# The deformable convolution of an eight-stage image network: a tap's spread products in row groups, and a new order of the stage

## The chip, the cores and the metric

The kernel runs on 1 core of one Trainium2 chip. The metric is the device time of one execution in microseconds. Before the change it is 1125.55 us, the median of 3 runs (1121.36 to 1129.44). Engines are named as the profile names them: PE is TensorE, DVE VectorE, ACT ScalarE, POOL GpSimd, SP SyncE.

## What is computed

Sixteen images of 16 x 16 pixels with 64 channels go through eight stages, each a residual on a normalized input. The change is in the third, a deformable 3 x 3 convolution. Its core in the reference:

```
om = lax.conv_general_dilated(x, om_kernel, (SH, SW), 'SAME', ...) + om_bias
off = om[..., :2 * DG * K].reshape(Bx, Ho, Wo, DG, K, 2)
mask = jax.nn.sigmoid(om[..., 2 * DG * K:]).reshape(Bx, Ho, Wo, DG, K) * 2.0
...
for yi, wy in ((y0, 1.0 - fy), (y0 + 1.0, fy)):
    for xi, wx in ((x0, 1.0 - fx), (x0 + 1.0, fx)):
        ...
        g = jnp.take_along_axis(xf, lin[..., None], axis=1)
        val = val + g * (wy * wx * valid.astype(x.dtype))[..., None]
cols = (val * mask_t[..., None]).reshape(Bx, Ho * Wo, K * Cx)
out = jnp.matmul(cols, kernel).reshape(Bx, Ho, Wo, -1) + bias
```

Each output pixel reads the image at nine shifted places (taps), each between four pixels. The other stages are a gate, a top-k feed-forward, three mixtures of experts, an attention and a plain 3 x 3 convolution whose kernel is divided by its spectral norm. That norm comes from 20 steps of a power iteration, of which each block of the third stage carries one.

## The kernel before

The images are worked in eight blocks of two images (512 pixels), in every stage. The code issues to each engine by hand, in the order in which it stands, and the engines meet at semaphores. `trips` runs a stage's body as a loop of three rounds of two blocks (u = 0 and 1) and a last round apart (wrap). While block b is worked, block b + 1 is prepared and the normalization of block b + 2 is begun.

The third stage gathers without addresses. For a tap, a pixel's weight on source pixel (y, x) is a product of two hats, max(0, 1 - |distance|) in y and in x. `hats_distances` (DVE) forms the distances for 16 rows and 16 columns, `hats_form` (ACT, L869 and L871) takes absolute value and hat, `hats_masked` multiplies the mask in. `hats_part` (ACT, L876), `hats_rest` and `hats_last` split the result into three bf16 parts in HB. `turn` (PE, L1265) turns two taps of HB, pixels to the free side, into bank 7; `ht_out` (ACT, L887) copies them to HT: 96 rows, three parts of 16 for y and three of 16 for x.

Then three products per tap spread a tap's 16 values to 256 source pixels: `spread_y` (L1273) makes two of 128 x 512 in a pair of banks, `spread_x` (L1269) one in bank 0. All three contract the same 96 rows against a 0/1 matrix `spread`. `xr_out` (ACT, L893) copies bank 0 to XR, `products` (DVE, L1902) multiplies the pair by XR into S. `gather` (PE, L1281) contracts S over the source pixels with Z, the image already multiplied by the tap's kernel (`z_tile`, L1257, copied by `z_out`, L881), and sums nine taps in bank 1. At a block's end the offsets of block b + 2 are made (`offsets`, L1236), copied (`offsets_out`) and turned (`turn_offsets`, L1242); the output is biased (L1948), turned back (`turn_output`, L1249) and added to X (L1950), which is block_done.

Two pairs of banks (2 and 3, 4 and 5) serve the y products, the z tiles and the offsets. Which pair a tap takes is a table:

```
TAP_PAIR = (1, 1, 0, 0, 1, 1, 0, 0, 1)
Z_PAIR = (1, 0, 1, 0)
```

PE spreads a tap in two steps, `tap(k)` for the y products and `x_of(k + 1)` for the next x product, with gathers, turns and z tiles between them, and the border of a block spreads tap 0 and the x part of tap 1 ahead. Between them stand `slot1`, `slot2` and `slot3` (L1096 to L1121), the small products of the power iteration, whose rest runs on POOL: `seg1`, `seg2`, `seg3`, `front` and, in even blocks, `split_later`, which splits weights for later stages.

## Time and profile before

| | us |
|---|---|
| median of 3 runs (lowest, highest) | 1125.55 (1121.36, 1129.44) |
| the profiled execution | 1133.36 |
| its span, first to last instruction | 1131.6 |
| PE busy | 933.4 (82%) |
| DVE busy | 695.3 (61%) |
| ACT busy | 492.1 (43%) |
| POOL busy | 444.7 (39%) |
| mean granted clock | 0.862 |

The profile is one execution. Times in its rows are microseconds from the span's start, where not marked ns. A share of busy time averages over eight stages with different limits. The third stage lies at about 230 to 530 us. Matmuls are pipelined: a record's duration contains the way through the array, so the starts of neighbours tell how long one held the engine. PEclk is the granted clock of TensorE as a share of its full speed. An f32 product appears as two records.

### The profile page before, as it was taken

What the parts mean: (1) busy time and instruction counts of PE and PEld (TensorE: products, weight loads), DVE (VectorE), ACT (ScalarE), POOL (GpSimd) and SP (SyncE); (2) the same over time, 40 slices, a digit from 0 to 9 for tenths busy, and PEclk for the clock granted to TensorE, in tenths of its full rate; (3) what the DMA queues carried; (4) which work ended last, traced back from release to release, by engine and by line L of the source; (5) the groups of instructions that cost most, each with busy time, mean ns of one, the idle gap of its engine ahead of it and who ended that gap; (6) DMA issues with size and microseconds to landing.
All of it is one profiled execution on the core that took longest, in us unless ns stands there. A gap on an engine that the chain in (4) does not pass through costs nothing.

```text
span 1131.6 us, 16666 instructions
## 1 busy us (share of the span) xinstructions
PE 933.4 (82%) x4266; PEld 558.4 (49%) x4266; DVE 695.3 (61%) x2439; ACT 492.1 (43%) x966; POOL 444.7 (39%) x1234
## 2 busy tenths in 40 slices
PE   2766486758999889889999976899897768999998
PEld 2655354545554545455444444556554544445443
DVE  2887677736455654564388857665875555656642
ACT  1324122246445653563266644343441013666664
POOL 4666566621542546336444401243555221111100
PEclk9999996559888988999799988776977666999999
DMA  4500000000000000000000000000000000000000
GB/s 74 91 1 1 1 1 0 0 1 1 1 1 0 0 0 0 0 1 1 1 1 1 0 1 0 1 1 0 0 1 1 0 0 1 6 5 9 5 6 9
DMA packets 26352, 6.21 MB, mean 5 GB/s; under 512 B 24068, under 2 KB 26244, under 8 KB 26308
## 3 DMA queue, kind: packets, MB, share of 16 engines
q1 hardware_dynamic: 26308, 5.70, 2.9%
q8 instruction: 18, 0.29, 0.1%
q14 instruction: 26, 0.21, 0.1%
HBM read 4.65 MB, written 1.05 MB: 5 GB/s over the span
## 4 chain that ended last, share of the span: by engine, by line
PE 51%; DVE 12%; issue 7%; ACT 3%; POOL 3%; DVEq 0%; POOLq 0%; ACTq 0%; another core or an unknown queue 0%
PE banks L1455 10%; PE banks L1281 6%; PE banks L1165 6%; PE banks L1166 4%; PE banks L1472 3%; PE banks L1096 3%; PE banks L1479 3%; PE banks L1423 2%; PE banks L1273 2%; DVE weighted L2007 2%; DVE V L1730 2%; DVE summed L2011 2%; PE banks L1429 1%; PE banks L1236 1%; PE banks L1269 1%
## 5 line engine op out<-in xcount | busy, mean ns | idle before, releaser
L646 POOL TENSOR_TENSOR rstd<-vareps,neghalf 128x4 f32<-128x4 f32 x64 | 66.8, 1044 | 274.4 <-DVE vareps L1714 269.5
L969 ACT ACTIVATE scratch<-banks,b 128x512 f32<-128x512 f32 x224 | 143.3, 682 | 52.5 <-PE banks L1166 39.9
L1455 PE MATMUL banks<-scratch,W 128*64 128x512 f32 (+1 forms) x448 | 149.3, 649 | 2.3 <-DVE weighted L2007 2.0
L1902 DVE TENSOR_TENSOR scratch<-banks,XR 128x1024 f32<-128x1024 f32 x72 | 87.5, 1224 | 87.4 <-PE banks L1273 61.1
L1165 PE MATMUL banks<-VS,W_hi 128*128 128x512 f32 x240 | 116.3, 485 | 2.1 <-DVE X L2083 1.0
L1166 PE MATMUL banks<-VS,W_lo 128*128 128x512 f32 x240 | 102.6, 427 | 0.0
L2007 DVE SCALAR_TENSOR_TENSOR weighted<-banks,b,cwide 128x512 f32<-128x512 f32 x72 | 54.0, 750 | 75.6 <-PE banks L1455 74.0
L1281 PE MATMUL banks<-scratch,region 128*64 128x256 f32 x576 | 87.4, 429 | 3.0 <-DVE scratch L1902 3.0
L980 ACT ACTIVATE cwide<-banks 128x512 f32<-128x512 f32 x96 | 57.5, 599 | 66.7 <-PE banks L1472 66.3
L1730 DVE TENSOR_SCALAR V<-X,moments,rstd 128x64 f32 (+1 forms) x256 | 67.7, 328 | 24.7 <-POOL rstd L646 22.0
L1165 PEld LDWEIGHTS banks<-VS,W_hi 128*128 128x128 f32 x240 | 49.1, 205 | 50.7 <-issue 26.1
L1139 PE MATMUL banks<-ident,V 128*128 128x128 f32 x128 | 34.3, 359 | 46.5 <-DVE V L1730 46.3
L742 ACT ACTIVATE VS<-banks 64x256 fp32r<-64x256 f32 x96 | 36.4, 379 | 77.5 <-PE banks L1139 61.2
L574 POOL TENSOR_TENSOR cp<-U,qv 64x18 f32<-64x18 f32 x40 | 8.1, 221 | 142.7 <-ACT U L800 142.7
L1281 PEld LDWEIGHTS banks<-scratch,region 128*64 128x64 f32 x576 | 38.0, 148 | 37.5 <-issue 22.3
L1757 DVE TENSOR_TENSOR VS<-banks,VS 64x256 fp32r<-64x256 f32 x96 | 40.5, 422 | 21.4 <-ACT VS L742 19.5
L1139 PEld LDWEIGHTS banks<-ident,V 128*128 128x128 f32 x128 | 16.4, 170 | 75.3 <-issue 42.1
L1455 PEld LDWEIGHTS banks<-scratch,W 128*64 128x64 f32 (+1 forms) x448 | 32.9, 150 | 40.7 <-issue 27.8
L1166 PEld LDWEIGHTS banks<-VS,W_lo 128*128 128x128 f32 x240 | 49.9, 208 | 6.1
L1472 PE MATMUL banks<-cwT,select 16*128 16x512 f32 x96 | 50.8, 529 | 0.8 <-ACT cwT L974 0.8
L2011 DVE TENSOR_TENSOR summed<-summed,weighted 128x512 f32<-128x512 f32 x72 | 49.9, 693 | 2.5
L887 ACT ACTIVATE HT<-banks 96x1024 bf16<-96x1024 bf16 (+1 forms) x40 | 37.2, 931 | 29.0 <-PE banks L1265 29.0
(289 smaller groups left out, 2008.3 us busy)
## 6 DMA issues: line engine op xcount, KB each, us to landing
W<-in_L_ffn_W SPq DMA_DIRECT2D x3, 512.0 KB
X<-in_x SPq DMA_DIRECT2D x8, 128.0 KB, 2.6
out<-X SPq DMA_DIRECT2D x8, 128.0 KB, 2.0
cwide<-in_L_ffn_W SPq DMA_DIRECT2D x2, 256.0 KB
KC<-in_L_conv_kernel SPq DMA_DIRECT2D x2, 144.0 KB
W<-in_L_ffn_W SPq DMA_DIRECT2D x1, 256.0 KB
cwide<-in_L_ffn_w SPq DMA_DIRECT2D x2, 128.0 KB
Ko<-in_L_conv_w SPq DMA_DIRECT2D x1, 144.0 KB, 3.7
```

The costliest lines, as they stand in the source:

```text
L646: pool.tensor_tensor(rstd[:], vareps[:], neghalf[:], ALU.pow).then_inc(rstd_ready, 1)
L969: act.activation(hid[:, c % 4, :], bank[c % 2][:, :], ACT.Gelu, bias=b1[s][:, w:w + 1]).then_inc(h_ready, 1)
L980: act.activation(cwide[:, j, :], bank[4][:, :], ACT.Copy).then_inc(wide_copied, 1)
L1165: pe.matmul(out, hi, VS[u][:], start=True, stop=False)
L1166: return pe.matmul(out, lo, VS[u][:], start=False, stop=True)
L1281: ins = pe.matmul(bank[1][m * C:(m + 1) * C, 0:PIX], Z[v][:, 2 * m + h, k * C:(k + 1) * C], S[:, k % 3, h, m * PIX:(m + 1) * PIX], start=( ...
L1455: ins = pe.matmul(y, W2[s][:, w, :], hid[:, c % 4, :], start=opens, stop=closes, skip_group_check=True)
L1472: pe.matmul(bank[4][:, :], select[:, j, :], cwT[:], start=True, stop=True).then_inc(wide_psum, 1)
L1730: ins = vec.tensor_scalar(V[u][:, place, :], X[:, bass.ds(b * NT + t, 1), :].rearrange("p o c -> p (o c)"), moments[:, t, 0:1], rstd[:, t: ...
L1902: vec.tensor_tensor(S[:, k % 3], pair(p), xr, ALU.mult).then_inc(s_ready, 1)
L2007: vec.scalar_tensor_tensor(weighted[:] if j else summed[u][:], bank[2 + j % 2][:, :], b2[s][:, j:j + 1], cwide[:, j, :], ALU.add, ALU.mult ...
L2011: add = vec.tensor_tensor(summed[u][:], summed[u][:], weighted[:], ALU.add)
```

## The change

The hats lie in four groups instead of two: y rows 0 to 7, y rows 8 to 15, x 0 to 7, x 8 to 15, each with three parts of 8 and a gap of 8 to make 32. HB and HT so have 128 rows, of which the gaps are filled with zeros once, on ACT. `spread` is one matrix of 128 x 128. A tap's three products now contract different rows: y's first half rows 0 to 31, the second 32 to 63, x rows 64 to 127. They are issued together (`spread_tap`), two taps ahead of the gather, and tap k takes the pair (u + k) % 2, as does the z tile that follows it. The offsets and the turned offsets go to bank 7. At the program's start POOL makes the grids with eight iotas of eight columns where there were four of sixteen, and `spread` with twelve selects where there were nine. `slot1` and `slot2` are cut in two parts with a gather between them. The orders of PE, ACT, DVE and POOL are rewritten; the border spreads taps 0, 1 and 2 of the next block (9, 10 and 11 in the code). The buffers `rest`, `weighted` and `summed` share one piece of memory.

The diff, cut, with eight spaces of the code's indent taken out:

```
-spread = sb("spread", [HAT, 3, P], BF16)
+spread = sb("spread", [P, P], BF16)
...
-hats = sb("hats", [P, 2, NT * TAPS, IMG])
-rest = sb("rest", [P, 2, NT * TAPS, IMG])
+hats = sb("hats", [P, 4, NT * TAPS, HALF])
+sums = sb("sums", [P, 3 * BLK])
+rest = view(sums, 0, (4, NT * TAPS, HALF))
 offs = sb("offs", [P, NT, 2 * TAPS])
-HB = [sb(f"HB{u}", [P, NT * TAPS, HAT], BF16) for u in range(2)]
-HT = sb("HT", [HAT, 2, 2, BLK], BF16)
+HB = [sb(f"HB{u}", [P, NT * TAPS, P], BF16) for u in range(2)]
+HT = sb("HT", [P, 2, 2, BLK], BF16)
...
-weighted = sb("weighted", [P, BLK])
-summed = [sb(f"summed{u}", [P, BLK]) for u in range(2)]
+weighted = sums[:, 0:BLK]
+summed = [sums[:, (u + 1) * BLK:(u + 2) * BLK] for u in range(2)]
...
-TAP_PAIR = (1, 1, 0, 0, 1, 1, 0, 0, 1)
...
+    by_pixel = spread[:].rearrange("r (y x) -> r y x", x=IMG)
     for q in range(PARTS):
-        for half_y in range(2):
-            v = spread[:, half_y, :].rearrange("r (y x) -> r y x", x=IMG)
+        for h in range(2):
+            link(pool.affine_select(out=by_pixel, in_=by_pixel, compare_op=ALU.not_equal, fill=1.0,
+                                    base=-(QUAD * h + HALF * q), pattern=[[-1, HALF], [0, IMG]],
+                                    channel_multiplier=1))
+            v = by_pixel[:, :, HALF * h:HALF * (h + 1)]
             link(pool.affine_select(out=v, in_=v, compare_op=ALU.not_equal, fill=1.0,
-                                    base=-IMG * q - 8 * half_y, pattern=[[-1, 8], [0, IMG]],
+                                    base=-(QUAD * (2 + h) + HALF * q), pattern=[[0, HALF], [-1, HALF]],
                                     channel_multiplier=1))
-        v = spread[:, 2, :].rearrange("r (y x) -> r y x", x=IMG)
-        link(pool.affine_select(out=v, in_=v, compare_op=ALU.not_equal, fill=1.0,
-                                base=-IMG * (PARTS + q), pattern=[[0, 8], [-1, IMG]],
-                                channel_multiplier=1))
...
-            if s != 2 and first_half:
+            if s == 2:
+                front()
+            if first_half:
                 seg1(step)
+            if u == 0 and s == 2:
+                rewind()
+                split_later(i, s, wrap)
             if first_half:
                 seg2(step)
             if second_half:
                 seg3(step)
             if second_half:
-                if not (s == 5 and wrap):
+                if s == 0 or s == 2 and wrap and u == 1 or s in (1, 5) and not wrap:
                     front()
                 rewind()
-            if u == 0 and s in (2, 6):
+            if u == 0 and s == 6:
...
+        for u in range(2):
+            gaps = HB[u][:].rearrange("p n (a r) -> p (n a) r", a=4)[:, :, PARTS * HALF:]
+            act.activation(gaps, ones[:, 0:1].rearrange("p (n o) -> p n o", o=1).to_broadcast([P, 4 * NT * TAPS, QUAD - PARTS * HALF]),
+                           ACT.Copy, scale=0.0)
...
-    def spread_x(k, slot):
-        pe.matmul(bank[0][:, :], spread[:, 2, :], HT[:, slot, k % 2, :], start=True, stop=True).then_inc(xr_psum, 1)
-    def spread_y(k, slot, p):
-        for h in range(2):
-            ins = pe.matmul(pair(p)[:, h, :], spread[:, h, :], HT[:, slot, k % 2, :], start=True, stop=True)
-        ins.then_inc(yr_psum, 1)
+    def spread_tap(slot, j, p):
+        quads = ((slice(0, QUAD), pair(p)[:, 0, :]), (slice(QUAD, 2 * QUAD), pair(p)[:, 1, :]),
+                 (slice(2 * QUAD, 4 * QUAD), bank[0][:, :]))
+        for q, (rows, out) in enumerate(quads):
+            ins = pe.matmul(out, spread[rows, :], HT[rows, slot, j, :], start=True, stop=True)
+            if q:
+                ins.then_inc((None, yr_psum, xr_psum)[q], 1)
...
+            def spread_on(k):
+                turned, j = (k // 2, k % 2) if k < TAPS else (5 + (k - TAPS) // 2, (k - TAPS) % 2)
+                pe.wait_ge(ht_ready, g + (turned + 1))
                 pe.wait_ge(xr_ready, n + k)
-                spread_x(k, (5 * u + k // 2) % 2)
+                pe.wait_ge(s_ready, n + (k - 2 + 1 + 3))
+                if more and k in (3, 5, 7, 9):
+                    pe.wait_ge(z_copied, z + (k - 1) // 2)
+                spread_tap((5 * u + turned) % 2, j, (u + k) % 2)
...
-            turn_pair(1)
-            tap(1)
-            x_of(2)
             pe.wait_ge(block_done, b + (NB * s + CREDIT))
             gather(n, 0, u)
-            slot1(step, bank[6])
-            tap(2)
+            if more:
+                pe.wait_ge(emask_ready, b + 2)
             turn_pair(2)
-            x_of(3)
+            if more:
+                z_next(0, 1)
+            slot1(step, bank[6], 0)
             gather(n + 1, 1, u)
-            if more:
-                z_next(0, 1)
-            tap(3)
-            x_of(4)
+            slot1(step, bank[6], 1)
+            spread_on(3)
+            spread_on(4)
             gather(n + 2, 2, u)
-            tap(4)
             turn_pair(3)
...
             gather(n + 8, 8, u)
             if not wrap:
                 pe.wait_ge(vp_ready, b + 3)
-                pe.wait_ge(z_copied, z + NT)
+                pe.wait_ge(ht_ready, g + 7)
                 offsets(u)
-                pe.wait_ge(omt_ready, b + 3)
+            if more:
+                spread_on(11)
             pe.wait_ge(yt_ready, b + 1)
             turn_output(bank[1][:, PIX:2 * PIX])
             if not wrap:
+                pe.wait_ge(omt_ready, b + 3)
                 turn_offsets()
```

The rest of the reordering is shown as it stands in the built programs. `[waits ...]` names the semaphores an instruction waits for. First PE at the border of two blocks, from the offset products (L1236, in the changed kernel L1247) on. L1249 and L1260 turn the output, L1242 and L1253 the offsets, L1265 turns hats, L1273 is the y spread, L1281 and L1292 the gather, L1283 the spread of a tap. Before:

```order
L1236 MATMUL banks<-VP,OMK_cols 64x512 [waits z_copied]
L1236 MATMUL banks<-VP,OMK_cols 64x512 x8
L1415 REGISTER_ALU [waits omt_ready]
L1249 MATMUL banks<-ident,yt 128x2x64 [waits yt_ready]
L1249 MATMUL banks<-ident,yt 128x2x64
L1242 MATMUL banks<-fold_quads,omt 128x32 x4
L1265 MATMUL banks<-identb,HB 96x128 [waits ht_ready]
L1265 MATMUL banks<-identb,HB 96x128 x7
L1336 REGISTER_ALU
L1273 MATMUL banks<-HT,spread 128x512 [waits s_ready]
```

Now:

```order
L1247 MATMUL banks<-VP,OMK_cols 64x512 [waits ht_ready]
L1247 MATMUL banks<-VP,OMK_cols 64x512 x8
L1348 REGISTER_ALU [waits xr_ready,ht_ready]
L1283 MATMUL banks<-HT,spread 128x512 [waits s_ready]
L1283 MATMUL banks<-HT,spread 128x512 x2
L1420 REGISTER_ALU
L1260 MATMUL banks<-ident,yt 128x2x64 [waits yt_ready]
L1260 MATMUL banks<-ident,yt 128x2x64
L1253 MATMUL banks<-fold_quads,omt 128x32 [waits omt_ready]
L1253 MATMUL banks<-fold_quads,omt 128x32 x3
L1292 MATMUL banks<-scratch,region 64x256 [waits s_ready,block_done]
L1292 MATMUL banks<-scratch,region 64x256 x3
```

The gather of the new block (L1292) came after a turn, two y products and an x product, and comes now right behind the turned offsets. Three spread products stand behind the offset products, and the output is turned before the wait on omt_ready.

Second, PE in the middle of a block: y products (L1273), x product (L1269), the preparation's turn (L1139), gather (L1281). Before:

```order
L1257 MATMUL banks<-KC_lo,VS 128x288
L1336 REGISTER_ALU
L1273 MATMUL banks<-HT,spread 128x512 [waits s_ready]
L1273 MATMUL banks<-HT,spread 128x512
L1344 REGISTER_ALU
L1269 MATMUL banks<-HT,spread 128x512 [waits xr_ready,ht_ready]
L1375 REGISTER_ALU
L1137 REGISTER_ALU [waits vt_ready,ch_act]
L1139 MATMUL banks<-ident,V 128x128 [waits v_ready]
L1139 MATMUL banks<-ident,V 128x128
L1281 MATMUL banks<-scratch,region 64x256 [waits s_ready]
L1281 MATMUL banks<-scratch,region 64x256 x3
```

Now, gather 3 (L1292) and taps 5 and 6 (L1283):

```order
L1292 MATMUL banks<-scratch,region 64x256 [waits s_ready]
L1292 MATMUL banks<-scratch,region 64x256 x3
L1350 REGISTER_ALU [waits s_ready,xr_ready,ht_ready]
L1283 MATMUL banks<-HT,spread 128x512 [waits z_copied]
L1283 MATMUL banks<-HT,spread 128x512 x2
L1346 REGISTER_ALU
L1348 REGISTER_ALU [waits xr_ready,ht_ready]
L1283 MATMUL banks<-HT,spread 128x512 [waits s_ready]
L1283 MATMUL banks<-HT,spread 128x512 x2
```

What stood spread among gathers stands now in pairs of taps, with no other product between the two; the second waits for xr_ready and s_ready.

Third, ACT at the start of a block: HT copy (L887), XR copy (L893), T for the power iteration (L791), z copy (L881), hats (L869, L871). Before:

```order
L887 ACTIVATE HT<-banks 96x1024 [waits ht_psum]
L891 ISA
L893 ACTIVATE XR<-banks 128x512 [waits s_ready,xr_psum]
L789 ISA
L791 ACTIVATE T<-banks 64x10 [waits ch_pe]
L791 ACTIVATE T<-banks 64x2x4
L886 REGISTER_ALU
L887 ACTIVATE HT<-banks 96x1024 [waits ht_psum]
L891 REGISTER_ALU
L893 ACTIVATE XR<-banks 128x512 [waits s_ready,xr_psum]
```

Now:

```order
L887 ACTIVATE HT<-banks 128x1024 [waits ht_psum]
L880 ISA
L881 ACTIVATE region<-banks 128x576 [waits z_psum]
L868 ISA
L869 ACTIVATE hats<-hats 128x1152 [waits dist_ready]
L871 ACTIVATE hats<-hats 128x1152 [waits dist_abs]
L789 ISA
L791 ACTIVATE T<-banks 64x10 [waits ch_pe]
L791 ACTIVATE T<-banks 64x2x4
L891 ISA
L893 ACTIVATE XR<-banks 128x512 [waits s_ready,xr_psum]
```

The z copy and the two hats activations stood behind two XR copies and two HT copies; now they stand ahead of the block's first XR copy, which follows T.

DVE has the same instructions: the hats' distances stand ahead of product 2, the normalization behind it, and the products of taps 9 and 10 (0 and 1 of the next block) at the end, one on each side of the bias (L1948). POOL takes the preparation's rstd first and then front(), seg1 and, in even blocks, split_later.

## Rows read from the trace of the kernel before

**Rows 1.** Busy time in the eight blocks: window, PE, PEld, DVE, ACT, POOL busy, PEclk, DMA, GB/s
```profile
262.00:293.60 31.60, 28.48 (x189) 16.34 (x185) 17.66 (x27) 17.90 (x32) 10.29 (x38) 0.95 0.00 1
293.60:330.50 36.90, 33.59 (x205) 19.50 (x204) 20.45 (x38) 19.49 (x35) 17.47 (x62) 0.86 0.01 1
330.50:369.30 38.80, 35.02 (x205) 19.70 (x205) 20.43 (x38) 19.50 (x35) 14.23 (x55) 0.82 0.00 0
369.30:402.50 33.20, 29.14 (x204) 16.94 (x203) 20.53 (x37) 19.50 (x35) 18.14 (x62) 1.00 0.00 0
402.50:439.50 37.00, 33.52 (x205) 19.15 (x204) 20.35 (x38) 19.50 (x35) 14.13 (x54) 0.86 0.00 0
439.50:478.30 38.80, 35.06 (x205) 19.93 (x205) 20.54 (x38) 19.49 (x35) 17.72 (x62) 0.82 0.00 0
478.30:508.10 29.80, 26.46 (x198) 15.79 (x198) 20.37 (x37) 18.29 (x33) 11.54 (x47) 1.00 0.01 1
508.10:530.40 22.30, 20.40 (x147) 10.85 (x145) 10.70 (x10) 10.01 (x19) 13.31 (x54) 1.00 0.00 1
```

**Rows 2.** Grouped lines of the stage, 262 to 530 us: busy, mean ns | idle before, releasers
```profile
L1902 DVE TENSOR_TENSOR scratch<-banks,XR 128x1024 f32<-128x1024 f32 x70 | 85.1, 1224 | 79.5 <-PE banks L1273 53.2 <-ACT XR L893 21.7 <-DVE hats L1874 2.2
...
L893 ACT ACTIVATE XR<-banks 128x512 f32<-128x512 f32 x70 | 41.5, 593 | 9.8 <-PE banks L1269 9.4
...
L887 ACT ACTIVATE HT<-banks 96x1024 bf16<-96x1024 bf16 (+1 forms) x38 | 35.2, 926 | 26.1 <-PE banks L1265 26.1
L1269 PE MATMUL banks<-HT,spread 96*128 96x512 bf16 x69 | 28.7, 417 | 14.8 <-ACT XR L893 10.9 <-ACT HT L887 4.0
```

**Rows 3.** Timeline in a block at full clock: start, duration us; spread y, spread x, gather
```profile
390.21 0.61 PE L1273 MATMUL banks<-HT,spread 96*128 96x512 bf16 x2
...
390.65 0.38 PE L1269 MATMUL banks<-HT,spread 96*128 96x512 bf16 x1
...
390.96 1.08 PE L1281 MATMUL banks<-scratch,region 128*64 128x256 f32 x8
```

**Rows 4.** Timeline and windows outside the stage: full-row products, then half-row products of the attention
```profile
537.45 2.08 PE L1429 MATMUL banks<-before,ident 128*128 128x512 f32 x2
...
537.40:541.30 3.90, 3.90 (x12) 2.37 (x12) 0.00 (x0) 0.00 (x0) 3.42 (x7) 0.50 0.00 0
...
678.25 1.14 PE L1546 MATMUL banks<-VM 64*128 64x256 f32 x8 [0.24 <-ACT VM L762]
...
678.20:679.20 1.00, 0.95 (x8) 0.90 (x10) 0.69 (x2) 0.00 (x0) 0.00 (x0) 1.00 0.00 0
```

**Rows 5.** Timeline over the border of blocks 2 and 3, PE
```profile
364.89 2.53 PE L1236 MATMUL banks<-VP,OMK_cols 128*64 128x512 f32 x9
...
368.27 0.43 PE L1249 MATMUL banks<-ident,yt 128*128 128x128 f32 x2 [0.85 <-ACT omt L856]
...
371.40 0.39 PE L1269 MATMUL banks<-HT,spread 96*128 96x512 bf16 x1 [0.68 <-ACT HT L887]
...
371.72 1.08 PE L1281 MATMUL banks<-scratch,region 128*64 128x256 f32 x8
```

**Rows 6.** Timeline of the same block: second hats activation, XR copy, next x product
```profile
378.93 1.16 ACT L871 ACTIVATE hats<-hats 128x1152 f32<-128x1152 f32 x1
...
380.00 0.58 ACT L893 ACTIVATE XR<-banks 128x512 f32<-128x512 f32 x1
...
380.72 0.38 PE L1269 MATMUL banks<-HT,spread 96*128 96x512 bf16 x1 [0.90 <-ACT XR L893]
```

**Rows 7.** Windows just before the clock fell, in block 0
```profile
277.10:280.50 3.40, 3.12 (x23) 2.23 (x23) 2.61 (x6) 1.43 (x7) 0.00 (x0) 1.00 0.00 0
290.80:294.10 3.30, 2.45 (x15) 1.53 (x14) 0.68 (x3) 0.68 (x1) 2.79 (x9) 1.00 0.00 0
```

**Rows 8.** Timeline of POOL at the start of the program
```profile
8.23 0.82 POOL L496 TENSOR_SCALAR_AFFINE_SELECT spread<-spread 96x128 bf16<-96x128 bf16 x2
...
13.06 0.29 POOL L626 TENSOR_SCALAR vb<-vb 64x1 f32<-64x1 f32 x1 [0.66 <-DMA gcol<-in_L_ffn_wr]
```

More of the change, by code:

```diff
@@ L1091, in last_bias, with times @@
                 ins.then_inc(set_pe, 1)
-            def times(weights, vec, at):
-                for j in range((TAPS + 1) // 2):
+            def times(weights, vec, at, part=None):
+                two = (TAPS + 1) // 2
+                for j in {None: range(two), 0: range(2), 1: range(2, two)}[part]:
                     n = min(2, TAPS - 2 * j)
@@ L1232, in offsets @@
             def offsets(v):
[L1234 removed]
+                om = bank[7][0:2 * QUAD, :]
                 for k in range(TAPS):
```

250 lines of the change are left out of this document (119 added, 131 removed).

## The prediction

> **What bounds the kernel now.** I read the page first: PE is busy 82% of the span, DVE 61%, ACT 43%, and most of the chain that ended last runs over PE. So a stage is paid at the pace of PE's queue, plus what PE waits for inside it. The change touches the third stage, so next I cut that stage at the ends of its eight blocks [rows 1]. Blocks 1 to 5 do the same work but take 36.9, 38.8, 33.2, 37.0 and 38.8 us. What differs is the granted clock of TensorE (1.00 is 2.4 GHz, 0.50 the lower level, 1.2 GHz): 1.00 in the block of 33.2 us, 0.86 and 0.82 in the others. A mean of 0.86 over 36.9 us is 10.3 us at the lower of the two levels, 0.82 over 38.8 us is 14.0 us. Such a block pays 3.7 or 5.6 us for them, 0.36 to 0.40 us for each low microsecond. The last two blocks ran at full clock; block 6 forms no new offsets, block 7 prepares nothing. DVE is busy about 20.4 us in each full block and ACT 19.5, so neither fills a block, but both stand in PE's way by their order.
>
> The grouped lines of the stage [rows 2] give the partners: a product on DVE 1.22 us, a copy of the x rows (XR) on ACT 0.59 us, and 14.8 us in which PE stood before the x product of a tap, 10.9 of them for an XR copy.
>
> **The spread products.** At full clock the two y products of a tap start 0.44 us before its x product, 0.22 us each, and the x product holds PE 0.31 us until the gather starts [rows 3]: 0.22 of its own and 0.09 for the change of shape (128 columns to 64). A tap costs 0.65 us plus that change. Now the three stand on rows 0 to 31, 32 to 63 and 64 to 127. Do such products run side by side? The stage never does it, but the attention does with two halves: eight records of 256 columns on 64 rows take 1.14 us at clock 1.00, where two records of 512 columns on all rows take 2.08 us at 0.50, so 1.04 us at full clock [rows 4]. Eight of 256 are twice the columns of two of 512, for about the same time: halves in different rows run together. I take 0.25 us for a tap (0.22 and the weight load in front), 0.40 saved, over nine taps 3.6 us a block. The bounds are 3.6 (all three together) and -1.6 (all one after another, with 0.09 us for two more changes of shape in each of nine taps).
>
> The Trainium skill, TensorEngine Tiling (Array Packing), Key Properties, says that changing the tiling mode, and not just the tile, drains the engine. The 0.09 us of the gather agrees for a change of column width [rows 3]; no row shows 32-row products beside 64-row ones. That is the third rival.
>
> **The block border.** In the block at full clock PE goes from the start of the offset products to the next gather in 6.83 us [rows 5]. Two waits are in it: 0.85 us for the offsets' copy and 0.68 us for the turned hats' copy on ACT; the turn and the y and x products of the next taps stand in it too. In the new order tap 2 of the next block is spread behind the offset products, the output is turned before the offsets' copy is waited for, and the gather comes at once; the turn stands behind it. The copy ends about when the output is turned, so I leave 0.3 us of wait; the turn and the spreads move inside the block and cost there what they cost here. I take -1.2 us a block (bounds 0 and -1.5).
>
> **The new waits.** XR comes out of a single bank. The next x product can start only when the copy is out: 0.38 us of product [rows 3], 0.59 of copy [rows 2], 0.14 until PE starts [rows 6], 1.1 us. Before, a gather, a turn or a z product stood between two x products. Now taps 3 and 4, 5 and 6, 7 and 8, 9 and 10 stand together with nothing between, and the three products of a tap share one queue place. So the second of each pair costs 1.1 - 0.25 = 0.85 us of wait, 3.4 us in four pairs. At two of them ACT has work in front of the copy. Copy 3 stands behind the hats' two activations (1.16 us each), which wait for DVE's distances: that pattern alone held PE 0.90 us in the block before [rows 6]. Copy 7 stands behind a cast of the hats as long. I add 0.65 us at each: 4.7. The XR waits of before, 10.9 us over the seven blocks that prepare another [rows 2], are 1.6 a block, so the net is +3.1 us (bounds 0, if the second of a pair is hidden by what PE still has to do, and 4.7). Further, spread 5 waits for the copy of a z tile that stands behind the preparation's copy, and the second turn for the first turn's copy out of the same bank, 0.93 us in the mean [rows 2]. I take one such copy for both, +0.9 (bounds 0 and 1.9). DVE's order costs nothing: gather 2 needs product 2, and both stand behind the hats' distances as copy 3 does, which holds spread 4 longer.
>
> The Trainium skill, TensorEngine Tiling (Array Packing), PSUM Bottleneck, warns that a copy out of PSUM may become the bottleneck once the products are faster. The 10.9 us of XR waits say the same of this kernel [rows 2]; by that rule alone the saving would be gone, and my sum has most of it gone.
>
> At full clock a block then takes 33.2 - 3.6 - 1.2 + 3.1 + 0.9 = 32.4 us.
>
> **The clock.** It fell after stretches in which PE worked through small products or stood still. 277.1 to 280.5 held the second group of power-iteration products (ten records of two columns); 290.8 to 294.1 held the border, PE busy 2.45 of 3.3 us [rows 7]. The new border is denser, and both groups of ten are cut by a gather: two causes are weakened. But the nine taps stream for 0.25 us instead of 0.65 and PE stands six times a block, most clearly between spreads 3 and 4, around 5 and 6 with the small products behind, and between 7 and 8. I expect the falls to move there, not to go: as many low microseconds as now, 9.7 a block (the mean of blocks 1 to 5). They cost less, since part lies on waits that ACT sets: 0.31 us each (bounds 0 and 0.40), 3.1 us. The block is then 35.5 us.
>
> **Start of the program.** POOL makes nine selects from 8.23 us on and then stands 0.66 us for a DMA, until 13.06 [rows 8]: they end at 12.40, 0.46 us each. There are now twelve of them, half of smaller size, and eight iotas of half size for four. That is about +1.6 us, of which 1.0 shows (bounds 0.6 and 1.9). The cost at nothing: two fills of the gaps in HB on ACT, hidden by the offset products before the stage's first copy (as large as a hats activation, so 2.3 us without that cover), the hats in four parts of eight for two of sixteen (same elements in each instruction), POOL's front() behind rstd (POOL idles half of the stage [rows 1]; 1 us a block if seg1 became late for PE), the shared buffer (no stage uses both).
>
> **The sum.** Blocks 1 to 5: 5 x (35.5 - 36.94) = -7.2. Block 0 with the start of the stage: +1 (it had almost no low clock and no border to save). Block 6: +1 for the same reason. Block 7: -0.5, nine taps saved against four pairs of waits. Start of the program: +1.0. Together -4.7 us. The profiled execution took 1133.36 us (span 1131.6), 7.8 above the median of the three runs; the same -4.7 on 1125.55 gives 1121 us.
>
> **Rivals.**
> First, the clock stays up: with the border dense and the small products cut, it does not fall in the stage. Blocks 1 to 5 take 32.4 us: 5 x -4.54 = -22.7; block 0 -2, block 6 -0.3, block 7 -0.5, start +1.0: -24.5, 1101 us. For it: both kinds of stretch before a fall are reworked. Against: PE's column time sinks and its waits grow.
> Second, slower, one mechanism: the lower clock holds through the middle of every block, because the short spreads with a wait behind each give PE too little to do from spread 3 to the third turn. With 22 low microseconds a block at 0.31 each it takes 32.4 + 6.8 = 39.2 us: 5 x 2.3 = +11.3, block 0 +4, block 6 +4, block 7 +1, start +1: +21, 1146 us. It decides from (36.94 - 32.4) / 0.31 = 14.6 low microseconds a block, half again what there is now.
> Third, the row groups do less than they should: the 64-row product waits until the two 32-row ones have drained. A tap then costs 0.55 us for 0.25, at five of nine taps on the path (elsewhere the XR copy is later anyway): +1.5 a block, 33.9 at full clock; PE streams more, so say 8 low microseconds, 36.4: 5 x -0.5, and the edges and the start as above, +3.5: +1, 1126 us.
>
> **Chances.** The forecast 0.38, the clock stays up 0.27, the clock falls more 0.20, the groups drain 0.15. About 1% (11 us) is what a measurement of this kernel can tell from no change. The forecast's own spread is wide beside that (per block 1.5 us either way is 10 us): of its 0.38 I give 0.12 to faster by over 1%, 0.20 to within, 0.06 to slower. Of the third rival 0.02, 0.10 and 0.03. With the first all faster and the second all slower: 0.41, 0.30, 0.29. The range takes both outer cases: with all bounds favourable about 1090, with the second rival 1147.
>
> **What would show it.** Right: the three spread products of a tap start within 0.03 us of each other and the next tap's x product some 1.1 us later, with PE idle for XR about 5 us a block; the second product on DVE no longer waits for the y products; POOL's last select ends near 14 us. A third product 0.3 us behind the first two would be the third rival. Clock 1.00 in most blocks of about 32.5 us is the first, 0.7 or lower with blocks of 39 us the second. The forecast is wrong altogether if a full-clock block takes less than 30 us (then the XR copy is no bound) or more than 35.

## The result, and the profile after

The changed kernel takes 1151.05 us (median of 4 runs, 1148.24 to 1155.66), the kernel before 1126.51 us (4 runs beside it, 1121.36 to 1129.44). The ratio is 1.020, with a 95% interval of 1.016 to 1.024: slower, by some 24 us, where 1121 us was forecast with a range up to 1147. The time is close to that of the second rival (1146 us).

The profiled executions lie 15.8 us apart (1149.14 and 1133.36 us; spans 1147.4 and 1131.6), less than the medians: that of before lay 7 us above its median, that of after 2 below its own. The traces account for the 15.8; no trace shows the other 9 or so. Where a median and a ratio differ in the table further down, the ratio decides, since it leaves disturbed executions out. "Low microseconds" below are, as in the prediction, time at the lower of TensorE's two levels: a window's length times 2 x (1 - PEclk).

The busy time of the eight blocks of the third stage after the change, cut at the same instruction as [rows 1] (window, length, then PE, PEld, DVE, ACT, POOL busy, PEclk, DMA share, GB/s):

```profile
262.50:303.20 40.70, 36.83 (x209) 21.66 (x209) 19.08 (x28) 20.65 (x36) 16.50 (x57) 0.75 0.00 1
303.20:342.20 39.00, 34.96 (x205) 20.38 (x204) 20.25 (x37) 20.05 (x35) 14.48 (x53) 0.78 0.00 1
342.20:379.90 37.70, 33.14 (x204) 19.40 (x204) 20.55 (x37) 20.05 (x35) 18.91 (x61) 0.82 0.00 0
379.90:417.30 37.40, 33.53 (x204) 20.14 (x204) 20.23 (x37) 20.05 (x35) 14.47 (x53) 0.82 0.00 0
...
454.80:492.40 37.60, 33.05 (x203) 19.25 (x203) 20.24 (x37) 20.05 (x35) 14.47 (x53) 0.82 0.00 0
492.40:524.00 31.60, 26.05 (x189) 15.53 (x188) 19.95 (x37) 18.74 (x33) 17.84 (x65) 0.95 0.00 1
524.00:547.40 23.40, 20.04 (x143) 11.31 (x143) 9.38 (x9) 8.74 (x17) 9.62 (x41) 0.93 0.01 1
```

Read the PEclk column first. Before, one full block of five had 1.00 and two had 0.86; now all five have 0.78 to 0.82, which is 13.5 to 17.2 low microseconds each, 14.3 in the mean (9.7 before). Blocks 1 to 5 together take 189.2 us, before 184.6: only 4.6 us more. The larger part sits ahead of them. Block 0 ran at clock 0.95 before and now at 0.75 (3.2 and 20 low microseconds). From the stage's first offset product to the end of block 0 it takes 70.7 us where it took 63.5: +7.2. Blocks 6 and 7 add 1.8 and 1.1 us, the way to the stage 2.3, and all that follows the stage gives 1.2 back. That is 15.8.

The grouped lines of the stage, which answer to [rows 2] (busy, mean ns of one | idle before, releasers):

```profile
L1911 DVE TENSOR_TENSOR scratch<-banks,XR 128x1024 f32<-128x1024 f32 x70 | 85.1, 1217 | 74.9 <-ACT XR L893 62.8 <-issue 9.7 <-DVE sums L1892 1.6
L1283 PE MATMUL banks<-HT,spread 32*128 32x512 bf16 (+1 forms) x207 | 53.1, 416 | 30.7 <-ACT XR L893 23.1 <-issue 5.5 <-ACT region L881 2.1
L893 ACT ACTIVATE XR<-banks 128x512 f32<-128x512 f32 x70 | 41.8, 597 | 48.4 <-PE banks L1283 48.3
```

DVE's product no longer waits for the y products; it waits 62.8 us for the XR copy, that copy 48.3 us for PE, and PE 23.1 us for the copy (10.9 before). The three now stand in one ring.

**Are the three products side by side?** The weight loads show it: the first load of this spread stands at 424.21 us and its first product at 424.22. They stand in the timeline of PE's loads at full clock in block 4 (start, duration us):

```profile
424.21 0.10 PEld L1283 LDWEIGHTS banks<-HT,spread 32*128 32x128 bf16 x2 [1.52 <-issue]
424.54 0.09 PEld L1283 LDWEIGHTS banks<-HT,spread 64*128 64x128 bf16 x1 [0.23 <-issue]
424.86 0.14 PEld L1292 LDWEIGHTS banks<-scratch,region 128*64 128x64 f32 x2 [0.23 <-issue]
```

The two 32-row products start together (one group of two, whose loads take 0.10 us in all where one takes 0.09). The 64-row one comes 0.33 us behind them (0.32 in spread 3, two microseconds earlier), and the gather 0.32 behind that: 0.65 us from the first start to the gather, where it was 0.75 [rows 3]. This is the pattern that the third rival named. At half clock the same step is 0.54 us (254.26 to 254.80 in the stage's first tap). The x product is the late one of the three, and it is the one whose copy everybody waits for.

**The pairs.** The timeline of block 3, PE and ACT, around spreads 3 and 4 and spreads 5 and 6:

```profile
384.55 1.16 ACT L871 ACTIVATE hats<-hats 128x1152 f32<-128x1152 f32 x1
384.89 0.71 PE L1283 MATMUL banks<-HT,spread 32*128 32x512 bf16 x3
385.98 0.60 ACT L893 ACTIVATE XR<-banks 128x512 f32<-128x512 f32 x1
...
386.81 0.71 PE L1283 MATMUL banks<-HT,spread 32*128 32x512 bf16 x3 [1.22 <-ACT XR L893]
...
392.34 0.71 PE L1283 MATMUL banks<-HT,spread 32*128 32x512 bf16 x3
393.09 0.60 ACT L893 ACTIVATE XR<-banks 128x512 f32<-128x512 f32 x1 [1.19 <-PE banks L1283]
...
393.92 0.71 PE L1283 MATMUL banks<-HT,spread 32*128 32x512 bf16 x3 [0.87 <-ACT XR L893]
```

Spread 6 starts 1.58 us behind spread 5: 0.75 until the copy starts, 0.60 of copy, 0.23 until PE starts. Spread 4 starts 1.92 us behind spread 3, since copy 3 stands behind the second hats activation and T. Over blocks 1 to 5, PE's waits after and before (us in total, times, longest):

```profile
PE banks L1283 <- ACT XR L893: 19.3, 20, 1.2
PE banks L1283 <- ACT region L881: 1.4, 2, 0.7
```

```profile
PE banks L1269 <- ACT XR L893: 7.8, 10, 0.9
PE banks L1249 <- ACT omt L856: 4.0, 5, 0.8
PE banks L1269 <- ACT HT L887: 2.6, 5, 0.7
PE banks L1281 <- DVE scratch L1902: 2.3, 5, 0.5
PE banks L1115 <- DVE VS L1757: 1.4, 5, 0.3
```

Exactly four waits a block for the XR copy, 3.9 us, in place of two that made 1.6. All the other waits of before, 2.1 us a block, are gone or nearly so.

**The border** behind block 4, at full clock (PE):

```profile
450.59 2.53 PE L1247 MATMUL banks<-VP,OMK_cols 128*64 128x512 f32 x9
453.05 0.71 PE L1283 MATMUL banks<-HT,spread 32*128 32x512 bf16 x3
...
455.06 1.08 PE L1292 MATMUL banks<-scratch,region 128*64 128x256 f32 x8
```

From the offset products to the gather it is 4.47 us, where it was 6.83 [rows 5], and PE waits for nothing in it.

**The start.** POOL's last select ends at 14.53 us, and what stands behind it starts 1.69 us later than the same row of [rows 8]; the stage's first offset product on PE (last row) came at 230.11 before:

```profile
14.24 0.29 POOL L497 TENSOR_SCALAR_AFFINE_SELECT spread<-spread 128x64 bf16<-128x64 bf16 x1
14.75 0.23 POOL L623 TENSOR_SCALAR vb<-vb 64x1 f32<-64x1 f32 x1 [0.22 <-POOL spread L497]
...
232.50 4.07 PE L1247 MATMUL banks<-VP,OMK_cols 128*64 128x512 f32 x9 [1.12 <-issue]
```

### The profile page after: what moved, and what is told of

The parts are those of the page before. It is cut to its first block, busy times and chain, and to the rows that moved or that the text cites. A ratio compares the mean times of both kernels' runs of the same rounds, so it can differ in the third digit from the quotient of the medians.

```text
span 1147.4 us, 16701 instructions
## 1 busy us (share of the span) xinstructions
PE 942.2 (82%) x4266; PEld 565.9 (49%) x4266; DVE 694.0 (60%) x2439; ACT 498.3 (43%) x968; POOL 450.4 (39%) x1241
## 4 chain that ended last, share of the span: by engine, by line
PE 53%; DVE 11%; issue 7%; ACT 4%; POOL 1%; DVEq 0%; POOLq 0%; ACTq 0%; another core or an unknown queue 0%
PE banks L1461 10%; PE banks L1292 7%; PE banks L1176 6%; PE banks L1283 4%; PE banks L1177 4%; PE banks L1478 3%; PE banks L1276 3%; PE banks L1485 2%; PE banks L1104 2%; PE banks L1429 2%; DVE sums L2020 2%; PE banks L1247 2%; DVE sums L2024 2%; DVE V L1736 2%; ACT XR L893 1%
## 5 line engine op out<-in xcount | busy, mean ns | idle before, releaser
L2020 DVE SCALAR_TENSOR_TENSOR sums<-banks,b,cwide 128x512 f32<-128x512 f32 x96 | 72.0, 750 | 94.0 <-PE banks L1461 89.9
L1292 PE MATMUL banks<-scratch,region 128*64 128x256 f32 x576 | 94.5, 459 | 1.0 <-DVE X L1963 1.0
L1283 PE MATMUL banks<-HT,spread 32*128 32x512 bf16 (+1 forms) x216 | 56.3, 423 | 31.8 <-ACT XR L893 23.1
L893 ACT ACTIVATE XR<-banks 128x512 f32<-128x512 f32 x72 | 43.0, 597 | 49.7 <-PE banks L1283 49.5
L1292 PEld LDWEIGHTS banks<-scratch,region 128*64 128x64 f32 x576 | 40.8, 159 | 28.2 <-issue 17.0
L1283 PEld LDWEIGHTS banks<-HT,spread 32*128 32x128 bf16 (+1 forms) x216 | 14.0, 93 | 77.3 <-issue 72.6
L887 ACT ACTIVATE HT<-banks 128x1024 bf16<-128x1024 bf16 (+1 forms) x40 | 37.5, 938 | 33.2 <-PE banks L1276 33.0
```

The source lines that it names most:

```text
L893: act.activation(XR[:, k % 3, :], bank[0][:, :], ACT.Copy).then_inc(xr_ready, 1)
L1283: ins = pe.matmul(out, spread[rows, :], HT[rows, slot, j, :], start=True, stop=True)
L1292: ins = pe.matmul(bank[1][m * C:(m + 1) * C, 0:PIX], Z[v][:, 2 * m + h, k * C:(k + 1) * C], S[:, k % 3, h, m * PIX:(m + 1) * PIX], start=( ...
L2020: vec.scalar_tensor_tensor(weighted[:] if j else summed[u][:], bank[2 + j % 2][:, :], b2[s][:, j:j + 1], cwide[:, j, :], ALU.add, ALU.mult ...
```

## The experiments

Twelve kernels ran, each beside the kernel before. "Block" is the mean of blocks 1 to 5 in the profiled execution and "low" the low microseconds in one of them. A profiled execution need not lie at its kernel's median: that of e4 is 10 us below, that of e10 is 9 below, that of before 7 above.

| run | edit | median us | ratio to before (95%) | block us | low us |
|---|---|---|---|---|---|
| before | | 1126.5 | 1 | 36.9 | 9.7 |
| after | the change | 1151.1 | 1.020 (1.016, 1.024) | 37.8 | 14.3 |
| e1 | row groups alone, old order | 1141.2 | 1.013 (1.007, 1.020) | 35.5 | 7.5 |
| e2 | full rows, new order | 1111.4 | 0.987 (0.981, 0.993) | 33.8 | 0 |
| e3 | x product first | 1145.1 | 1.016 (1.007, 1.025) | 36.8 | 13.0 |
| e4 | unpaired | 1089.0 | 0.968 (0.961, 0.974) | 29.8 | 2.8 |
| e5 | unread products at four waits | 1107.1 | 0.980 (0.972, 0.988) | 32.7 | 1.4 |
| e6 | unpaired, x first | 1088.8 | 0.963 (0.956, 0.969) | 30.6 | 3.7 |
| e7 | unpaired, full rows | 1098.0 | 0.965 (0.955, 0.975) | 30.1 | 1.5 |
| e8 | unread products at spread 4 only | 1139.9 | 1.013 (1.008, 1.017) | 34.8 | 6.2 |
| e9 | unread products at 6 and 8 | 1123.5 | 0.996 (0.993, 1.000) | 34.1 | 6.1 |
| e10 | unpaired, unread products at 6 | 1098.4 | 0.977 (0.971, 0.982) | 30.0 | 2.2 |
| e11 | unpaired, three products on 64 rows | 1086.5 | 0.962 (0.956, 0.968) | 29.2 | 2.2 |
| e12 | three products on 64 rows, new order | 1116.4 | 0.992 (0.988, 0.996) | 34.1 | 6.8 |

**e1, the row groups alone in the old order.** On the kernel before, with the changed layout of the hats and the changed constants:

```diff
-spread_x: spread[:, 2, :], HT[:, slot, k % 2, :]
+spread_x: spread[2 * QUAD:, :], HT[2 * QUAD:, slot, k % 2, :]
-spread_y: spread[:, h, :], HT[:, slot, k % 2, :]
+spread_y: rows = slice(QUAD * h, QUAD * (h + 1)); spread[rows, :], HT[rows, slot, k % 2, :]
```

> The kernel before with one part of the change: the hats laid out in row groups, the two y products of a tap on rows 0 to 31 and 32 to 63, the x product on rows 64 to 127, each at its old place in the old order. Theory A (32-row products run side by side, a change between 32 and 64 rows or to full rows costs about 0.1 us): the pair of y products holds PE 0.32 us at full clock where it held 0.44, nine times a block, so about 1 us a block less at full clock, but PE then streams less and the clock falls more: 1120 to 1140 us, the granted clock at or below the 0.86 of before. Theory B (row groups as good as my sum had them, the order is what costs): 2 us a block less and no more low clock, 1108 to 1115 us. Either way the start of the program costs 1.5 us. If it comes out above 1140, the row groups alone carry the loss.

It took 1141 us. The blocks are of two kinds: blocks 2 to 5 are good, blocks 1 and 7 are not.

```profile
298.60:340.00 41.40, 38.64 (x204) 20.92 (x204) 20.63 (x37) 19.62 (x35) 18.40 (x66) 0.71 0.00 1
340.00:374.20 34.20, 30.04 (x205) 17.03 (x204) 20.28 (x37) 19.51 (x35) 13.55 (x54) 0.95 0.00 0
...
507.40:534.90 27.50, 25.50 (x147) 12.85 (x145) 10.70 (x10) 9.99 (x19) 13.26 (x53) 0.75 0.00 1
```

Four of the five middle blocks take 34.1 us with 3.4 low microseconds, while block 1 has 24 of them and block 7 has 14, where it had none [rows 1]. Theory A's time is exceeded by 1 us, and with it the line at 1140: by the ratio, the row groups alone bring a loss of 1.3% in the old order, about 15 us. The trace shows where a loss arises, not all of it: the two profiled executions lie only 4.9 us apart. Blocks 1 to 5 are together 6.9 us shorter (177.7 for 184.6), block 7 is 5.2 longer, block 0 with the start of the stage 3.3, block 6 1.3, the way to the stage 1.6.

**e2, full rows in the new order.** The same order and waits, with three matrices over 128 rows with zeros:

```diff
-ins = pe.matmul(out, spread[rows, :], HT[rows, slot, j, :], start=True, stop=True)
+ins = pe.matmul(out, spread[:, q, :], HT[:, slot, j, :], start=True, stop=True)
```

> The changed kernel with its three spread products over all 128 rows (three matrices with zeros where the other groups stand), everything else as changed: layout, order, waits. PE streams three times 0.22 us at full clock in place of 0.22 plus 0.10 plus 0.22. Theory A (the row groups save only 0.1 us a tap at full clock, and the streaming they take away lets the clock fall): same time or faster than the changed kernel, 1135 to 1150 us, with fewer low microseconds in blocks 1 to 5 than 14 a block. Theory B (the order and its waits for the XR copy make the loss): 8 x 1.0 us slower than the changed kernel, 1155 to 1162 us, same clock.

It came out 40 us faster than the changed kernel, below theory A's range and far from theory B's. With e1 this closes the square: the new order alone gains 15 us on the kernel before, the row groups alone lose 15, and both together lose 24. Two of its blocks, and PE's waits in five:

```profile
294.30:328.10 33.80, 28.80 (x204) 16.64 (x204) 20.08 (x37) 19.83 (x35) 14.41 (x53) 1.00 0.00 1
...
361.90:395.70 33.80, 28.76 (x204) 16.59 (x204) 20.06 (x37) 19.83 (x35) 14.40 (x53) 1.00 0.00 0
```

```profile
PE banks L1283 <- ACT XR L893: 18.8, 20, 1.1
```

All twenty waits for the XR copy are still there, as long as in the changed kernel, and the clock is 1.00 in every block (PE waits 1.2 us a block for two other copies besides). So the waits alone do not bring the clock down; the waits together with short spreads do. e4 and e7 below, without these waits, complete the comparison in low microseconds a block: 14.3 with waits and short spreads, 0 with waits and full rows, 2.8 with short spreads and no such waits, 1.5 with neither.

**e3, the x product first.**

```diff
-quads = (rows 0:32 -> y0), (rows 32:64 -> y1), (rows 64:128 -> x)
+quads = (rows 64:128 -> x), (rows 0:32 -> y0), (rows 32:64 -> y1)
```

> The changed kernel with the 64-row x product issued ahead of the two 32-row y products of a tap. The third product starts 0.32 us behind the first at full clock and 0.54 at half, so the XR copy can start that much earlier. If the wait of the second spread of a pair is set by that copy (XR theory), each of four waits a block of 0.97 us shrinks by 0.32 to 0.54: 1.3 to 2 us a block, 10 to 14 us in all, 1137 to 1142 us. If the second of a pair is held by something else (the hats' activations in front of copy 3, DVE), only two or three of them shrink: 1142 to 1148 us. If the clock eats what the waits give back: within 3 us of the changed kernel.

PE's waits for the copy fell from 19.3 to 14.1 us in five blocks. Three of four shrank from 0.87 to about 0.55 us, the 0.32 expected; the one at spread 4 stayed at 1.22, since copy 3 stands behind the hats there. The block is 1.1 us shorter at about the same clock (13.0 low), and 1145 us is in the middle expectation.

**e4, unpaired.** Three gathers move between the spreads of their pair, and for spreads 5 and 6 the second group of small products, no longer split:

```diff
                     spread_on(3)
-                    spread_on(4)
                     gather(n + 2, 2, u)
+                    spread_on(4)
...
                     spread_on(5)
-                    spread_on(6)
-                    slot2(step, bank[6], 0)
+                    slot2(step, bank[6])
+                    spread_on(6)
                     gather(n + 4, 4, u)
-                    slot2(step, bank[6], 1)
```

(spreads 8 and 10 likewise behind gathers 6 and 8)

> The changed kernel with a gather (or the whole second group of small products) between the two spreads of each pair: spread 3, gather 2, spread 4; spread 5, small products, spread 6, gather 4; spread 7, gather 6, spread 8; spread 9, gather 8, spread 10. XR theory: PE no longer waits 0.97 us four times a block, so 3 to 3.9 us a block less, and with fewer gaps the clock falls less: 1110 to 1125 us. DVE theory (the gathers wait for DVE's products, which come in pairs after XR copies): the wait moves to the gather behind, which then waits for scratch, and the time stays within 8 us of the changed kernel, 1143 to 1151 us. A clock that stays as low as now would leave 1125 to 1135.

It is 62 us faster than the changed kernel and 38 faster than the kernel before, beyond every expectation. A block at full clock, and PE's waits in blocks 1 to 5:

```profile
350.90:379.20 28.30, 27.19 (x204) 16.06 (x203) 20.06 (x37) 19.58 (x35) 14.62 (x53) 1.00 0.00 0
```

```profile
PE banks L1283 <- ACT region L881: 3.1, 5, 0.6
PE banks L1276 <- ACT HT L887: 2.4, 5, 0.6
```

Not one wait for the XR copy is left, and none has moved to the gathers: the DVE theory falls. At full clock the block takes 28.3 us. The mean block loses 8.0 us: 3.9 of waits, and 11.5 low microseconds at 0.39 us, which is 4.5 (the price is worked out under e5). The sum of the two is 0.4 too large, and the two waits above have grown by 0.8 us a block besides, so the split is rough.

**e5, unread products in the waits.** The output is unchanged; eight extra products a block write where the spread overwrites them, and the wait on s_ready moves ahead of them:

```diff
+if k in (4, 6, 8, 10):
+    for _ in range(2):
+        pe.matmul(pair((u + k) % 2)[:, 0, 0:400], identb[:], HT[:, ..., j, 0:400], start=True, stop=True)
 pe.wait_ge(xr_ready, n + k)
```

> The changed kernel with two more products of 400 columns, whose result nobody reads, ahead of each wait for the XR copy at spreads 4, 6, 8 and 10 (0.33 us at full clock beside a wait of 0.97 us); order and waits as changed. Theory A (the gaps let the clock fall, and the clock carries the loss): the granted clock of blocks 1 to 5 goes to about 1.00 as it did with full-row products, the blocks take 32 to 33 us in place of 37.8, and the time is 1110 to 1120 us, although more work is done. Theory B (the waits themselves are the loss, the clock a bystander): nothing is won, 1150 us or above. If clock 1.00 comes with blocks above 34 us, the price of a low microsecond is below the 0.3 us that I used.

The changed kernel with more work is 44 us faster, which is theory A, 3 us below its range:

```profile
359.40:391.60 32.20, 29.48 (x213) 16.66 (x212) 20.06 (x37) 19.69 (x35) 14.41 (x53) 1.00 0.00 0
423.80:458.70 34.90, 32.42 (x212) 18.09 (x211) 20.25 (x37) 19.90 (x35) 14.62 (x53) 0.90 0.00 0
```

This pair of rows, blocks 3 and 5, is the price of the clock: same instructions, 7.0 low microseconds, 2.7 us, so 0.39 each. The changed kernel agrees: (37.4 - 32.2) / 13.5 is 0.39, and its block 1 gives (39.0 - 32.2) / 17.2 = 0.40.

**e6, e7 and e10 on top of the unpaired kernel.** e6 puts the x product first as in e3, e7 uses full rows as in e2, e10 the unread products of e5 ahead of spread 6.

> A gather between the spreads of each pair, and the x product ahead of the y products. With the waits for the XR copy gone on PE, an earlier copy has nothing to give there: within 4 us of the unpaired kernel (1085 to 1093 us). If DVE's products, which wait 10.8 us for XR copies in five blocks of the unpaired kernel, hold the gathers, it is 3 to 6 us faster, 1083 to 1086.

> A gather between the spreads of each pair, and full-row spread products in place of the row groups. At full clock a tap's spread costs 0.10 to 0.11 us more without row groups: nine taps in eight blocks, 7.5 us. Theory A: the unpaired kernel has only about 3 low microseconds a block to win back, 1 us a block, so it comes out 0 to +6 us, 1087 to 1095 us. If the row groups were worth what my sum gave them (0.40 us a tap), it would be 25 us slower, 1114; if they are worth nothing, 1082 to 1089.

> The unpaired kernel with the two unread products ahead of spread 6, behind the second group of small products, where its clock still fell for 3.4 us in four of the blocks 0 to 6. They cost PE about 0.5 us a block (0.33 of columns and two changes of shape) and can save 3.6 x 0.39 = 1.4 us in blocks that have the fall: 0 to 6 us in all, 1083 to 1089 us. If the fall just moves: 4 us slower, 1093.

e6 equals e4: without waits for the copy, an earlier copy gives nothing. e7, by its ratio, cannot be told from e4 either: over the whole program, this order without row groups is as fast as with them. Its full-clock block is 29.3 us where e4's is 28.3, so at full clock the row groups are worth 1.0 us a block or 0.11 a tap:

```profile
413.50:442.80 29.30, 28.11 (x204) 16.67 (x204) 20.07 (x37) 19.68 (x35) 14.59 (x53) 1.00 0.00 0
```

e10 missed: its full-clock block costs 28.9 us (0.6 more), and four of the blocks 1 to 6 kept their low stretch of 3.4 us; its ratio is 0.977 beside 0.968. A gap that is not there is not worth filling.

**e8 and e9, one gap at a time.** As e5, with k in (4,) and in (6, 8).

> The changed kernel with the two unread products of 400 columns ahead of spread 4 alone. In its blocks the clock fell for the first time right after spreads 3 and 4 (388.5 us in block 3, 426.0 in block 4). If that one gap starts the whole chain (each low stretch followed by the next), one filler brings most of what four brought: 0 to 5 low microseconds a block, 1108 to 1122 us. If every gap makes its own low stretch, two of three stretches stay: 9 to 11 low microseconds, 1135 to 1145 us.

> The changed kernel with the unread products ahead of spreads 6 and 8, not 4. If the gap at spread 4 starts the chain: little won, 10 low microseconds or more a block, 1140 to 1150 us. If every gap makes its own: one stretch of 3.4 us stays (at spread 4), block 33.5 us, 1113 to 1122 us.

Both times fit "every gap makes its own low stretch": e8 1139.9, e9 1123.5 (1.5 us above its range). The blocks do not. e8 has 6.2 low microseconds a block for the 9 to 11 expected, e9 6.1 for 3.4. In four of e9's five blocks they lie in one stretch of 6.8 us, near the gap between spreads 3 and 4, the one not filled. But in three of these four blocks it begins as the gap begins, not after it. In block 1 spread 3 starts at 302.25 us, its record ends at 302.96 and spread 4 starts at 304.10; the windows on both sides of 303.0, and the one ahead of the fall at 337.1 in block 2, read

```profile
299.60:303.00 3.40, 3.36 (x25) 2.12 (x23) 3.21 (x10) 3.37 (x5) 2.81 (x11) 1.00 0.00 0
303.00:309.80 6.80, 5.70 (x27) 3.37 (x29) 2.68 (x4) 3.15 (x8) 3.01 (x15) 0.50 0.00 0
...
333.70:337.10 3.40, 3.40 (x26) 2.17 (x24) 3.22 (x9) 3.37 (x4) 2.85 (x11) 1.00 0.00 0
```

PE had hardly stood still when the clock fell: it had worked through a gather, small products of one or two columns and the first of the two spreads. In the changed kernel the eleven falls of blocks 1 to 5 do come in or behind gaps (PE busy 2.2 to 2.5 of the 3.4 us ahead of them). In e2 PE was no busier around spreads 3 and 4, and the clock stayed up through the block:

```profile
299.20:302.60 3.40, 2.29 (x14) 0.98 (x16) 2.31 (x6) 2.27 (x5) 2.52 (x14) 1.00 0.00 0
```

So a gap of PE is neither needed for a fall nor enough for one, and that each gap makes its own stretch is not shown.

e8's blocks range over all values, from 38.8 us at 0.78 to one at full clock,

```profile
306.00:344.80 38.80, 35.13 (x207) 20.10 (x206) 20.24 (x37) 20.02 (x35) 14.53 (x53) 0.78 0.00 1
...
413.90:446.30 32.40, 28.07 (x205) 16.34 (x205) 20.38 (x37) 19.70 (x35) 18.71 (x61) 1.00 0.00 0
```

and its blocks 0, 6 and 7 ran at a lower clock than those of the changed kernel. What decides in a given block whether the clock falls stays open; what a low microsecond costs does not.

**e11 and e12, three products on 64 rows.** The x product on rows 64 to 127, then both y products on rows 0 to 63, with zeros:

```diff
-rows 0:32 -> y0, rows 32:64 -> y1, rows 64:128 -> x
+rows 64:128 -> x, rows 0:64 (matrix 0) -> y0, rows 0:64 (matrix 1) -> y1
```

> The unpaired kernel with all three spread products of a tap on 64 rows: the x product on rows 64 to 127, then the two y products both on rows 0 to 63 (each with zeros for the other's 32 rows). If the third product of the changed kernel came 0.32 us late because 32-row and 64-row products do not overlap, the x product and the first y product now start together, the second y product 0.22 us later, and the next gather about 0.53 us after the first start in place of 0.64: 0.1 us a tap, 1 us a block, 5 to 8 us in all, 1081 to 1084 us. If products in different row halves do not overlap here either, the three take 0.65 us and it is as slow as with full rows: 1094 to 1100 us. The clock can spoil 5 us of this either way.

> The same three products on 64 rows in the changed kernel's own order, with its pairs. The XR copy starts after the first product, 0.32 us earlier at full clock, so the four waits of a block shrink from 0.97 to about 0.65 us; the taps are 0.1 us shorter. At the clock of the changed kernel that is 1.3 + 0.9 us a block, 15 us: about 1136 us. If shorter waits also let the clock rise, as the fillers did, 1110 to 1125; if less streaming lets it fall further, 1140 to 1150.

The loads of e11's first tap in the stretch, all of one size and hence one group, and the gather behind them:

```profile
355.45 0.12 PEld L1283 LDWEIGHTS banks<-HT,spread 64*128 64x128 bf16 x3
355.99 0.20 PEld L1292 LDWEIGHTS banks<-scratch,region 128*64 128x64 f32 x4 [0.42 <-issue]
```

0.54 us from the first load to the gather's, against 0.65 with the mixed sizes: x and the first y product overlap, the second y product follows. e11's full-clock block is 27.7 us, 0.6 below e4's (1.0 expected), and with 1086.5 us it is the fastest of all, though it cannot be told from e4 and e6. e12 gains 35 us on the changed kernel, as its middle expectation says. The block is 3.7 us shorter, and 7.5 low microseconds fewer at 0.39 (2.9 us) are most of that. But the shorter waits, which that expectation gives as the reason, are there at two places of four only. Spreads 6 and 10 wait 0.65 and 0.69 us; spread 4 waits 1.33, with copy 3 behind the hats' activation, and spread 8 waits 1.11, with copy 7 behind the cast of the hats. Together they are as long as before, 18.8 us in five blocks. Why the clock is higher there is not settled.

## Why the prediction was wrong, point by point

The step of the sum that failed is the clock term: "as many low microseconds as now, 9.7 a block", at "0.31 us each", and +1 for block 0 with the start of the stage. The runs showed 14.3 low microseconds at 0.39, which is 5.6 us a block for the 3.1 that stood there, and +7.2 for block 0 and the start, with 16 low microseconds more. The saving in the spreads was mis-sized too, but the errors beside it cancelled that one.

- **What bounds the kernel: right.** PE's pace, and the clock in it. The gains and losses of the twelve kernels in the third stage are read from PE's queue and its clock; in every kernel DVE and ACT stay near 20 us in each of blocks 1 to 5.
- **The spread products, -3.6 us a block: wrong, -1.0.** What failed in it is "I take 0.25 us for a tap". The half-row products that stood for it [rows 4] were all of one size, 64 rows. Products on 32 rows overlap each other and products on 64 rows overlap each other (e11), but a 64-row product behind 32-row ones starts 0.32 us late. A tap costs 0.65 us to the gather for 0.75 before (0.11 a tap by e4 and e7). This is the third rival's mechanism, to which I gave 0.15. The Trainium skill, TensorEngine Tiling (Array Packing), Key Properties, says that changing the tiling mode drains the engine; the 0.32 us here, against the overlap that e11 has with one size, agrees. I had cited it and let a row decide that did not show the mix.
- **The border, -1.2: right.** Both waits went, 1.53 us, and no new one came.
- **The XR waits, net +3.1: right in mechanism, +2.3 measured.** Four a block as said. The pitch of a pair is 1.58 us for my 1.1, since the x product is the late one, and the hats add 0.35 at spread 4 and nothing at spread 8, for the 0.65 each that I added. 3.9 us stand for my 4.7: a pitch too short and additions too large partly cancelled.
- **Other copies, +0.9: 0.3 measured in the changed kernel, 1.2 with full rows at full clock (e2).** What I left out is the other side: waits for a product (0.5 us a block) and for the preparation (0.3) went away with the new order.
- **A full-clock block, 32.4: right in sum, 32.2 (e5), 32.4 (e8).** That is luck, since the parts were not: the saving in spreads was too large by 2.6 us, and so was the growth of the waits. In e8's full-clock block PE is idle 4.3 us, in that of before 4.1 [rows 1]; I had 2.8 us more.
- **The clock: the step that decided.** "As many low microseconds as now, 9.7 a block" is 14.3, and "0.31 us each" is 0.39: 5.6 us a block where I had 3.1. My own rows had given 0.36 to 0.40 for the price; I lowered it to 0.31 because part of the low clock would lie on waits, and it stayed where it was. The point of decision that I gave as 14.6 low microseconds is at (36.94 - 32.2) / 0.39 = 12.2. Both sizes erred the same way. The places were named rightly: the falls of the changed kernel lie within 2.5 us of the starts of spreads 4, 6 and 8. Products in the waits there brought 14.3 low microseconds down to 1.4 (e5), 6.2 (e8) and 6.1 (e9). Why the clock falls in one block and not in the next stays open.
- **Block 0 with the start of the stage, +1: +7.2 measured.** "It had almost no low clock" was read as nothing to lose. It has 16 low microseconds more from the stage's start on, 6.3 us at 0.39. This alone is 6 of the 20.5 us by which the sum missed, -4.7 against 15.8; blocks 1 to 5 are 11.8 (4.6 for my -7.2).
- **Start of the program, +1.0: 1.7 at POOL,** and the stage is entered 2.4 us late.
- **The rivals.** The second, slower one came true in place and sign, with 14.3 low microseconds for its 22 at a price of 0.39 for its 0.31, together with the third, whose own sum was 1 us too high (the edges and the start add to +2.5, not to +3.5). The first, the clock stays up at 1101 us, is not what happened, but it is what the same order does once PE has something to stream in the waits: e5, 1107 us.
- **The range** ended at 1147 with the second rival's own estimate, and left out that the second and the third rival could hold together. By my own point of 14.6 low microseconds, 14.3 would not even have made the blocks slower; the price of 0.39 lay inside the bounds that I wrote (0 to 0.40), but the range was formed with 0.31. With the 15.8 us between the profiled executions it would have been 1141 us, inside the range; the medians lie 24.5 apart.

## What to carry to other kernels

When products are made shorter so that PE saves time, price what PE then stands still for, and the clock with it: here the same order ran 44 us faster with useless products in its four waits. Better than filling is to put a consumer between two producers that share one bank; that edit alone, a gather between the spreads of each pair, turned a loss of 2% into a gain of 3%, and it gains as much without any row groups (e7). Of row groups, use one size within a group of products that should overlap.

## What the runs showed that I had not expected

- Adding work made the kernel faster (e5: eight products more a block, and 1107 us for 1151), and so did taking the row groups away (e2).
- The lower clock costs nothing where PE is not the bound. Up to the third stage the changed kernel shows a clock of 0.83 and e1 one of 0.90, 79 and 46 low microseconds, and both take the same time for it within 0.7 us:

```profile
0.00:232.50 232.50, 144.42 (x538) 113.78 (x538) 160.87 (x738) 66.94 (x198) 142.32 (x483) 0.83 0.12 20
```

```profile
0.00:231.80 231.80, 146.18 (x538) 114.56 (x539) 161.00 (x739) 67.02 (x198) 141.65 (x483) 0.90 0.12 20
```

- Behind the stage, where the kernels do the same work (2113 records on PE in each), the rest of the program took 590.4 us in e2 and 601.2 in the kernel before, with about 164 and 185 low microseconds. So some 11 us between two kernels come from stretches that the edit does not touch, and a ratio of 1% says little about the edit until the blocks are looked at.
